# A recurrence on one core: the scaling of x and the final addition on Pool in place of VectorE

## What is computed

```python
h = silu(q_pool @ W1.T + b1)
gate = sigmoid(h @ W2.T + b2)[:, None, :]
# a wavelet split of v, each part times gate, and put together again: a = gate * v
first = v + a
...
xW = einsum('ntd,dh->nth', x, Wx) + b
next_h = tanh(prev_h @ Wh + xw)      # 256 times, one step after the other
...
x = x + first(x, cond)               # so x1 = x * (2 + gate)
out = x1 + recurrence(x1)
```

## Time and profile before

| | |
|---|---|
| median of 3 runs | 253.32 us (252.93 to 253.58) |
| the profiled execution | 253.53 us, its span 251.7 us |
| TensorE products, weight loads | 96%, 91% of the span |
| VectorE, ScalarE, Pool | 60%, 48%, 2% |

### The profile page before, as it was taken

How to read it: one execution, slowest core, us unless ns; L and a number is a source line. 1 busy time by engine, 2 the same in 40 slices (tenths; PEclk the granted TensorE clock), 3 DMA queues, 4 the chain that set the end, 5 groups by cost and what they waited for, 6 DMA issues and landing times.

```text
span 251.7 us, 10329 instructions
## 1 busy us (share of the span) xinstructions
PE 242.7 (96%) x4220; PEld 228.3 (91%) x4220; DVE 150.8 (60%) x780; ACT 121.2 (48%) x1026; POOL 4.0 (2%) x9
## 2 busy tenths in 40 slices
PE   6499999999999999999999999999999999999995
PEld 5488999999999999999999999999999999999874
DVE  3146666666666666666666666666666666655553
ACT  2024445555555555555555555555555555555553
POOL 0310000000000000000000000000000000000000
PEclk9659999999999999999999999999999999999998
DMA  6999520020202010020202002020201002020211
GB/s 179 388 388 384 185 86 3 6 83 1 87 3 86 4 62 27 4 86 1 86 3 86 5 6 82 3 86 1 87 3 62 28 3 86 4 86 1 86 44 44
DMA packets 10877, 18.59 MB, mean 74 GB/s; under 512 B 1037, under 2 KB 2894, under 8 KB 10830
## 3 DMA queue, kind: packets, MB, share of 16 engines
q1 hardware_dynamic: 9870, 17.37, 19.0%
q10 hardware_dynamic: 960, 0.56, 0.7%
HBM read 9.54 MB, written 8.39 MB: 71 GB/s over the span
## 4 chain that ended last, share of the span: by engine, by line
PE 94%; DMA 3%; ACTq 1%; issue 0%; DVE 0%; ACT 0%; DVEq 0%
PE bank L200 59%; PE bank L195 30%; DMA wh_sb<-in_wh 3%; PE bank L188 3%; PE bank L177 1%; PE bank L183 1%; ACTq L147 0%; ACTq L146 0%; ACTq L148 0%; DVE g_t L342 0%; DVE x L298 0%; ACT tanh_z L156 0%; DVE h_t L311 0%; ACT h L166 0%; ACT h_t L167 0%
## 5 line engine op out<-in xcount | busy, mean ns | idle before, releaser
L354 DVE TENSOR_TENSOR h<-h_t,h 128x32 f16<-128x32 f32 x510 | 94.9, 192 | 88.3 <-ACT h_t L167 87.6
L200 PE MATMUL bank<-h,wh_a 128*128 128x32 f16 x1530 | 145.0, 179 | 0.8 <-ACT h L166 0.2
L200 PEld LDWEIGHTS bank<-h,wh_a 128*128 128x128 f16 x1530 | 122.4, 110 | 13.0 <-ACT h L166 7.2
L195 PE MATMUL bank<-x,wx_sb 128*128 128x128 f32 x512 | 109.8, 308 | 0.3 <-DVE x L298 0.3
L200 PE MATMUL bank<-h,wh_b 128*128 128x32 f16 x765 | 109.1, 176 | 0.0
L200 PE MATMUL bank<-h,wh_c 128*128 128x32 f16 x765 | 109.0, 176 | 0.0
L166 ACT ACTIVATE h<-bank 128x32 f16<-128x32 f32 x255 | 50.4, 198 | 115.5 <-PE bank L200 113.5
L200 PE MATMUL bank<-h_t,wh_sb 128*128 128x32 f32 x510 | 103.6, 285 | 0.0
L195 PEld LDWEIGHTS bank<-x,wx_sb 128*128 128x128 f32 x512 | 75.6, 193 | 0.8 <-issue 0.7
L200 PEld LDWEIGHTS bank<-h_t,wh_sb 128*128 128x128 f32 x510 | 75.8, 188 | 0.0
L200 PEld LDWEIGHTS bank<-h,wh_b 128*128 128x128 bf16 x765 | 68.9, 96 | 0.4
(11 more groups left out here) (31 smaller groups left out, 19.6 us busy)
## 6 DMA issues: line engine op xcount, KB each, us to landing
x<-in_x SPq DMA_DIRECT2D x16, 512.0 KB, 11.4
out_dram<-h_t SPq DMA_DIRECT2D x15, 512.0 KB, 2.7
w_t<-in_w SPq DMA_DIRECT2D x1, 256.0 KB, 2.9
w_t<-in_w ACTq DMA_DIRECT2D x1, 256.0 KB, 6.4
wx_sb<-in_wx SPq DMA_DIRECT2D x1, 256.0 KB, 7.2
wh_sb<-in_wh ACTq DMA_DIRECT2D x1, 256.0 KB, 7.3
out_dram<-h_t SPq DMA_DIRECT2D x1, 256.0 KB, 2.1
out_dram<-h_t SPq DMA_DIRECT2D x2, 128.0 KB, 2.4
```

The source lines that it names most:

```text
L195: return nc.tensor.matmul(pre[c % 2][e][m][:, steps, :], wx_sb[:, k, m * P:(m + 1) * P], moving, start=False, stop=False, skip_group_check ...
L200: return nc.tensor.matmul(pre[t // CS % 2][s % 2][m][:, s // 2, :], weights[:, k, m * P:(m + 1) * P], h_part, start=start, stop=stop, skip ...
L354: nc.vector.tensor_tensor(h2[:, t % 2, m, :], h_t[:, m, t * B:(t + 1) * B], h1[:, t % 2, m, :], ALU.subtract).then_inc(h2_ready[m], 1)
```

## The change

`scale` and `add_out` move from VectorE's queue to Pool's, as they are. `scale_apart` stays. Pool does in each step what VectorE did after its subtractions, and so waits first for `h2_ready[1]`, the second subtraction of the step. It begins after its work on the split of wh and after `g_ready`. VectorE keeps only the two subtractions of a step. The last addition, too, is Pool's, after both halves of the last state.

```diff
@@ Pool
+            def scale(c, n):
+                if n == 0:
+                    pool.wait_ge(x_loaded[c], DMA)
+                k, first = n // 4, c * N + n % 4 * P
+                cols = x1[:, k, first:first + P].rearrange("p (s b) -> p s b", b=B)
+                nc.gpsimd.tensor_tensor(cols, cols, g_t[:, k, :].unsqueeze(1).to_broadcast([P, CS // 4, B]), ALU.mult)\
+                    .then_inc(x1_ready, 1)
+
+            def add_out(t):
+                cols = slice(t * B, (t + 2) * B)
+                nc.gpsimd.tensor_tensor(h_t[:, :, cols], h_t[:, :, cols], x1[:, :, cols], ALU.add)\
+                    .then_inc(out_ready, 1)
+
+            pool.wait_ge(wh_split, 1)
+            pool.wait_ge(g_ready, 1)
+            for t in range(T):
+                c, s = t // CS, t % CS
+
+                if t < T - 1:
+                    pool.wait_ge(h2_ready[1], t + 1)
+                if c == 0:
+                    scale(1 + s // PIECES, s % PIECES)
+                elif s % 2 == 1 and c + 2 < CHUNKS:
+                    scale(c + 2, s // 2)
+                if t % 2 == 0 and t >= 2:
+                    add_out(t - 2)
+            for m in range(HALVES):
+                pool.wait_ge(h_ready[m], T)
+            add_out(T - 2)
@@ VectorE
-            def scale(c, n):
...
-            def add_out(t):
...
-                if c == 0:
-                    if s < PIECES:
-                        scale(1, s)
-                    else:
-                        scale(2, s - PIECES)
-                elif s % 2 == 1 and c + 2 < CHUNKS:
-                    scale(c + 2, s // 2)
-                if t % 2 == 0 and t >= 2:
-                    add_out(t - 2)
-            for m in range(HALVES):
-                dve.wait_ge(h_ready[m], T)
-            add_out(T - 2)
```

More of the change, by code:

```diff
@@ L299, in scale_apart @@
                     .then_inc(x1_ready, 1)
-            def scale(c, n):
[L302 to L307, removed]
-            def add_out(t):
-                cols = slice(t * B, (t + 2) * B)
-                nc.vector.tensor_tensor(h_t[:, :, cols], h_t[:, :, cols], x1[:, :, cols], ALU.add)\
-                    .then_inc(out_ready, 1)
             nc.vector.memset(ones[:], 1.0).then_inc(ones_ready, 1)
```

## The result

The changed kernel takes 255.09 us (median of 5, 254.41 to 255.95) against 253.32. The ratio is 1.0072 (95% interval 1.0053 to 1.0092), so it is slower by 1.3 to 2.3 us.

A forecast was written before the change was run, and what follows sets the result against it. The prediction took a per-step loop through ScalarE and TensorE as the bound; first chunk 0.52, step 14 and its border 0.1, end 0.1 gave +0.7 us on 253.32: 254.0 us, range 253.4 to 256.3.

The forecast's parts named there:

- The border decides: Rival: Pool's operation takes 0.40 to 0.51 us and delays TensorE at 14 chunk borders; 254.5 to 256.3 us, chance 0.32.
- VectorE's relief is worth nothing: Removing 120 scales and 128 adds from VectorE saves 0 in span, since ScalarE releases each pair of subtractions.
- Pool's price: One scale or add on Pool takes 0.36 us: fixed part 0.10 from a one-column memset, the rest by columns.
- Pool's start: Pool's operation starts 0.08 us after the second subtraction that releases it.
- Usual step: Steps with one Pool operation cost 0; Pool meets the next pair only from 0.44 us, and costs from 0.51.
- The 0.08 of cover: Gap in a usual step between Pool's expected end at 152.06 and the next pair of subtractions at 152.14.
- Border: First step of chunks 1 to 14, where TensorE waits for the last scale before its bias product: cost 0, without cover.
- The rule: At the chunk borders, from 0.37 us on, each 10 ns of Pool's operation costs 14 x 10 ns.
- First chunk: Two Pool operations after step 6 hold up VectorE's pair and delay TensorE's fill: +0.52 us, once.
- End: The last add on Pool is 0.07 us longer and released a few hundredths later: +0.1 us.
- The convoy: Rival: above 0.51 us Pool holds the next first subtraction every step; 274 us at the upper price, chance 0.09.
- the upper price of 0.58: Highest price for one Pool operation, half of the 1.15 us for 512 columns, if short pieces cost much.

The follow-up runs named there:

- e8_spread_after: The changed kernel with the second input product of each chunk's last step moved to the next chunk's first step, the wait for the scaled chunk behind it; 251.83 us.
- e7_spread_before: The kernel before with the second input product of each chunk's last step moved to the next chunk's first step, the scaled-chunk wait behind it; 250.69 us.
- e1: The changed kernel with the 128 adds back on VectorE and the 120 scales still on Pool; 255.15 us, ratio 1.0069.
- e9: Against the kernel with only the scales on Pool: Pool waits for the second subtraction only in steps where it has a scale; ratio 1.0056 to the kernel before.
- e2_adds_only: The changed kernel with the 120 scales back on VectorE and the 128 adds still on Pool; ratio 1.0000.
- e5_more_reading: The changed kernel with TensorE's scaled-chunk wait behind the bias product, plus one more SBUF-reading Pool operation per step that nobody waits for; 267.8 us.
- e4_first_chunk_dve: The changed kernel with the 16 scales of the first chunk's steps back on VectorE; ratio 1.0044.
- e3_bias_first_again: The changed kernel with TensorE's wait for the scaled chunk moved behind the bias product of the chunk's first step, second comparison; ratio 1.0025.

## Why the prediction was right in part

The measured 255.09 us lies in the range (253.4 to 256.3), but not in the forecast's own part of it (253.6 to 254.3). The case that came true is the second rival, *The border decides* (254.5 to 256.3, chance 0.32). The range held because it took that rival in, not because the forecast was right.

- *VectorE's relief is worth nothing*: right. Usual steps take 0.888 us before and after, and e8_spread_after against e7_spread_before shows it again.
- *Pool's price* is the step that failed: 0.36 us taken, 0.454 measured. The slope was near: 64, 128 and 512 columns took 0.322, 0.454 and 1.152, so 2.1 ns a column between the first two. The fixed part was wrong. I took a memset's 0.10; from the first two rows it is 0.19. A one-column memset reads nothing and was no row for the fixed part of an operation with two inputs. The estimate of 0.32 from the Trainium skill's page (GPSIMD Engine Reference, Elementwise — side-by-side cycle accounting) was further off.
- *Pool's start*: 0.08 after the pair, as measured. That a wait without an operation adds 0.065 more (e1, e9) I had not seen; in the changed kernel it falls on the adds of the last two chunks and costs nothing there.
- *Usual step*: right in its cost of 0. With 0.454 us Pool ends just after the next pair has started (0.45 to 0.44 of room), and no subtraction outside the first chunk is longer. The 0.08 of cover that the prediction counted on was used up.
- *Border*: the mechanism and the place were right, the size not. The rule gave 14 x (0.454 - 0.37) = 1.2 us. Measured were 13 x 0.045 + 0.08 = 0.7. The product could start 0.04 later than I had read from the gaps of the timeline. (The rival's lower end doesn't add up either: 0.7 + 0.4 = 1.1 gives 254.4, not 254.5.)
- *First chunk*: +0.52 predicted and +0.55 measured, with two errors against each other, which is luck. Pool was slower: its two operations after step 6 took 0.86 together (23.86 to 24.72) and not 0.72, its scale after step 7 0.45 and not 0.36, together 0.23 more. But I let a held pair start afresh when Pool ends and end 0.37 later; in fact the first subtraction ends 0.05 after Pool and the pair 0.15 after it (24.87), which is 0.22 less. Step 5, which I had put at 0, took 0.02 more. That VectorE is held at all was right, and so was the row taken as its sign: g_t ends 0.05 after Pool's cast. The +0.1 I had added for step 14 was 0.03.
- *End*: +0.2, not +0.1: 0.17 for the add itself, 0.03 for its later start.
- *The convoy*: didn't come, but its condition (over 0.51 us) was too low. In e2_adds_only Pool's 0.455 us starts 0.145 after the pair, so it ends where an operation of 0.52 would, and nothing is held. A held pair ends 0.15 after Pool, and Pool starts 0.08 later, so by these two numbers and the step of 0.89 the convoy begins near 0.66 us of Pool's work per step (an estimate). At the upper price of 0.58 it would not have come. e5_more_reading has some 0.73 us per step and has the convoy.

The terms with their measured sizes give 0.65 + 0.55 + 0.2 = +1.4 us. The medians give +1.8 (1.3 to 2.3) in the first comparison and +1.4 in the second. What of the difference is the start of the kernel, which came at 17.94 and 19.19 us in two executions of the changed kernel, and what is chance, these runs don't tell.

## What to carry to other kernels

When an operation moves to a slower engine, don't ask how busy either engine is. List who waits for its result and how much room each of them has at that place; of 248 operations here 16 had a waiter without room (14 borders, step 8, the last add), and those made most of the price. The rest, some 0.2 us, came by the subtraction that two Pool operations in a row held up in the first chunk. Where a queue waits for a result before an instruction that doesn't need it, move the wait: here that brought the border step back from 0.93 to 0.89 us with the operation as slow as before. And take the fixed part of a price from a row with the same number of inputs.

## What the runs showed of the hardware

**TensorE's clock can stay down for the rest of the run.** Eight kernels have the long wait at step 8 (the step takes 1.53 us or more, not 1.20). In 15 of their 73 executions, in five of the eight kernels, the clock stayed down. In the kernels without it (the kernel before, e2_adds_only, e4_first_chunk_dve, e7_spread_before) it came in none of 97. The windows of e9_no_empty_wait show it (columns: stretch, busy us and count of TensorE, its loads, VectorE, ScalarE, Pool, then the granted clock, DMA share, GB/s), and TensorE's timeline what it did:

```profile
24.00:26.00 2.00, 1.84 (x38) 1.52 (x37) 1.10 (x6) 0.93 (x8) 0.91 (x2) 1.00 1.05 388
26.00:27.00 1.00, 0.70 (x9) 0.60 (x8) 0.55 (x3) 0.47 (x4) 0.55 (x2) 0.71 1.05 385
27.00:28.00 1.00, 1.00 (x12) 0.94 (x12) 0.03 (x1) 0.00 (x0) 0.36 (x1) 0.50 0.96 354
...
100.00:110.00 10.00, 10.00 (x115) 9.38 (x115) 3.54 (x19) 3.38 (x30) 1.37 (x3) 0.50 0.02 3
300.00:310.00 10.00, 10.00 (x115) 9.56 (x115) 3.21 (x17) 3.26 (x28) 1.82 (x4) 0.50 0.01 2
...
26.05 0.18 PE L220 MATMUL bank<-h,wh_a 128*128 128x32 f16 x1
26.52 1.01 PE L215 MATMUL bank<-x,wx_sb 128*128 128x128 f32 x3 [0.30 <-POOL x L149]
```

The clock falls from 2.4 to 1.2 GHz between 26 and 27 us, where TensorE waits from 26.05 to 26.52, and never comes back, though TensorE is then busy without a gap; a usual step takes 1.39 to 1.41 us instead of 0.89. In e3_bias_first_again the wait is at 24.81 to 25.31 and the clock falls between 26 and 27 us as well, so the fall need not come in the wait itself. The same wait stands in the changed kernel's profiled execution (24.96 to 25.45), and there the clock stayed at 2.4 GHz. In e10_first_chunk_pool the 16 scales on Pool are the only difference to the kernel before, and the clock fell in one of its 12 executions, which is little by itself. So the longer wait goes with it in these runs. But all eight kernels also have Pool's scales in the first chunk, and no run has the wait without them, so the wait isn't shown to be the cause. What decides whether the clock falls in a given execution, and why it doesn't rise again in this stage while it rose at 18 us in the kernel before, stays open. In the changed kernel it happened in 3 of 15 executions, each about 48% longer. That weighs far more than the 0.7%.

**Pool's reading and VectorE's two-input operations exclude each other**, and the held one ends 0.05 us after Pool. In the first chunk of the changed kernel it took 0.30 to 0.47 us instead of 0.19, and a memset on Pool held nothing (0.18 and 0.19). An overlap of 0.08 cost nothing (e2_adds_only). The other way round, Pool's reading operation in e5_more_reading that began 0.01 after a subtraction (21.87 and 21.86) took 0.36 us and not 0.32.

**An operation of VectorE with one input is held too, also by a memset.** It is the one that makes g_t, once, at the start. In the kernel before it runs from 13.61 to 13.90, and Pool's cast from 13.25 to 13.86: it ends 0.05 after the cast. In e5_more_reading two memsets follow the cast, and g_t takes 0.47 us, to 0.05 after the last of them:

```profile
13.46 0.47 DVE L368 TENSOR_SCALAR g_t<-tanh_z 128x64 f32<-128x64 f32 x1 [3.57 <-ACT tanh_z L195]
...
13.10 0.61 POOL L146 CAST wh_c<-wh_last 128x512 bf16<-128x512 f32 x1
13.64 0.15 POOL L161 MEMSET idle_a<- 128x64 f32 x1
13.73 0.15 POOL L162 MEMSET idle_b<- 128x64 f32 x1
```

So two inputs are not the condition for every VectorE operation. This is one execution, and no run here has g_t without Pool beside it.

**A wait on Pool without an operation behind it** makes the next operation start 0.065 us later (0.145 instead of 0.08 after its release; e1_scales_only and e2_adds_only against e9_no_empty_wait).
